# A decoder layer's rotary embedding: biases of queries and keys moved from TensorE products to a VectorE addition

## The reference

```python
def _rope(x):
    ...
    x_rot = jnp.concatenate([-x[..., d // 2:], x[..., :d // 2]], axis=-1)
    return x * jnp.cos(C) + x_rot * jnp.sin(C)
...
y = jnp.einsum('bte,fe->btf', x, W) + bias          # 16 heads of 32
q = _rope(proj(Wq, bq))
k = _rope(proj(Wk, bk))
v = proj(Wv, bv)
att = jnp.einsum('bhqd,bhkd->bhqk', q, k) / scale   # causal mask, softmax, times v, times Wo, + bo
...
x = x + self_attention(layernorm(x))
x = x + cross_attention(layernorm(x), ctx)          # q and output projections on rounded int8 values
x = x + experts(layernorm(x))                       # top 8 of 64, capacity 128
```

## Time and profile before

| | |
|---|---|
| median of three runs | 1581.28 us (1580.71, 1581.28, 1584.12) |
| profiled execution, its time | 1576.11 us |
| its span, first to last instruction | 1574.3 us |
| TensorE (PE) busy | 1423.6 us, 90% |
| VectorE (DVE) busy | 1134.7 us, 72% |
| ScalarE (ACT) busy | 971.0 us, 62% |
| GpSimd (POOL) busy | 673.4 us, 43% |
| chain that ended last | PE 66%, DMA 23% |
| granted TensorE clock, mean | 0.963 of full speed |

### The profile page before, as it was taken

How to read it: one execution, slowest core, us unless ns; L and a number is a source line. 1 busy time by engine, 2 the same in 40 slices (tenths; PEclk the granted TensorE clock), 3 DMA queues, 4 the chain that set the end, 5 groups by cost and what they waited for, 6 DMA issues and landing times.

```text
span 1574.3 us, 35702 instructions
## 1 busy us (share of the span) xinstructions
PE 1423.6 (90%) x11060; PEld 1074.5 (68%) x11060; DVE 1134.7 (72%) x3075; ACT 971.0 (62%) x3345; POOL 673.4 (43%) x655
## 2 busy tenths in 40 slices
PE   3689999999999999999999999999728888888895
PEld 2467777777777777777777777777516555555563
DVE  5568888888888888888888888888633444444453
ACT  3357777777777777777777777777614333333332
POOL 1012443534444434535344444344542545455556
PEclk9799999999999999999999999999859999999997
DMA  8771332222211110101100111100497999999964
GB/s 297 302 262 35 117 134 105 98 105 81 91 39 38 41 34 27 27 28 33 45 28 27 27 33 39 35 21 22 134 368 203 288 266 292 273 288 280 261 99 50
DMA packets 159882, 195.68 MB, mean 124 GB/s; under 512 B 39685, under 2 KB 122117, under 8 KB 159824
## 3 DMA queue, kind: packets, MB, share of 16 engines
q1 hardware_dynamic: 120912, 157.14, 30.4%
q0 software_dynamic: 38912, 37.87, 11.8%
HBM read 127.47 MB, written 130.29 MB: 164 GB/s over the span
## 4 chain that ended last, share of the span: by engine, by line
PE 66%; DMA 23%; issue 5%; DVE 3%; ACT 2%; POOL 1%; SPq 1%; POOLq 0%; DVEq 0%
PE bank L507 34%; DMA out<-x,slots 20%; PE bank L532 7%; PE bank L489 7%; PE bank L525 5%; PE bank L539 4%; PE bank L513 3%; PE bank L545 2%; PE bank L520 2%; DMA x_in<-in_x 1%; ACT probs L972 1%; PE bank L494 1%; POOL routed L1754 1%; DMA probsT<-in_kT_w 1%; DMA probsT<-in_oT_w 1%
## 5 line engine op out<-in xcount | busy, mean ns | idle before, releaser
L972 ACT ACTIVATE probs<-bank,small 128x128 f32<-128x128 f32 x1024 | 362.4, 378 | 51.2 <-DVE small L1276 47.9
L1754 POOL DMA_INDIRECT routed<-row,slots x248 | 253.4, 1022 | 132.8 <-issue 73.0
L1719 POOL TENSOR_TENSOR small<-small,half 128x1 f32<-128x1 f32 x96 | 54.5, 567 | 534.3 <-DVE small L1248 534.3
L1825 POOL DMA_INDIRECT out<-x,slots x128 | 198.6, 1551 | 193.3 <-DMA out<-x,slots 144.9
L972 ACT ACTIVATION_READ_ACCUMULATOR probs<-bank,small 128x1 f32 x1024 | 222.0, 217 | 0.0
L966 ACT ACTIVATE probsT<-bank 128x512 f32<-128x512 f32 x256 | 144.1, 612 | 102.3 <-PE bank L532 102.3
L1276 DVE TENSOR_REDUCE small<-bank 128x4 f32<-128x512 f32 x256 | 166.8, 683 | 32.3 <-PE bank L525 32.3
L532 PE MATMUL bank<-idf,probs 128*128 128x128 f32 x1024 | 146.6, 277 | 1.9 <-ACT probs L972 1.9
L1674 DVE TENSOR_SCALAR slots<-pairs 128x1 uint32<-128x1 f32 x128 | 13.7, 149 | 180.4 <-DMA out<-x,slots 176.8
L532 PEld LDWEIGHTS bank<-idf,probs 128*128 128x128 f32 x1024 | 122.0, 144 | 25.1 <-DVE probs L1285 3.0
L1206 ACT ACTIVATE xn<-bank 128x192 f32<-128x192 f32 x64 | 21.3, 332 | 149.3 <-PE bank L912 149.3
(11 more groups left out here) (244 smaller groups left out, 3845.7 us busy)
## 6 DMA issues: line engine op xcount, KB each, us to landing
w_gate_up<-in_w_gate SPq DMA_DIRECT2D x128, 192.0 KB, 3.6
w_gate_up<-in_w_up SPq DMA_DIRECT2D x128, 192.0 KB, 3.8
w_down<-in_w_down SPq DMA_DIRECT2D x128, 192.0 KB, 4.1
routed<-empty_row SPq DMA_DIRECT2D x4, 5120.0 KB, 22.8
x_in<-in_x SPq DMA_DIRECT2D x32, 256.0 KB, 2.6
ctx_sb<-in_ctxT_in SPq DMA_DIRECT2D x32, 256.0 KB, 3.0
x_res<-in_x SPq DMA_DIRECT2D x32, 256.0 KB, 2.6
out<-x SPq DMA_DIRECT2D x32, 256.0 KB, 2.0
```

Of the source, the lines that this page charges most:

```text
L972: last = act.activation(probs[:, g, j * P:(j + 1) * P], bank[:, b, j * P:(j + 1) * P], ACT.Exp, bias=negated[:, h:h + 1], **({"accum_out": ...
L1754: pool.indirect_dma_start(routed, bass.IndirectOffsetOnAxis(ap=slots_of(m)[:, k:k + 1], axis=0), row_of(m)[:, :], None, bounds_check=SLOTS ...
L1825: pool.indirect_dma_start(out.rearrange("b p (h c) -> (b p h) c", h=2), bass.IndirectOffsetOnAxis(ap=place_of[k % 2][:, half_:half_ + 1], ...
```

## The change

The bias goes into neither projection any more. In the setup each bias is loaded as one row spread over the 128 partitions and rotated for the 128 positions, into `turned_bias` (128x1024: queries, keys). In each tile's rotation the order of the products is turned round, and VectorE adds `turned_bias` to `rot` before the final sum. The rotation has five counted steps instead of four, so the counts of those who wait for it change. The selecting matrix, `bias_rows`, `pick`, their three DMAs, the four VectorE steps and GpSimd's cast go.

```diff
@@ load_biases (SyncE, setup)
-                sp.dma_start(xn2[:, :], biases).then_inc(s_bias, 16)
-                sp.dma_start(roped[:, 0:NB * P], bias_sel).then_inc(s_bias, 16)
-                sp.dma_start(pick[:, :], pick_t).then_inc(s_bias, 16)
+                for k, dst in enumerate((x1, x2)):
+                    sp.dma_start(dst[:, :], biases[k:k + 1].to_broadcast([P, D])).then_inc(s_bias, 16)
@@ project (TensorE)
-                steps = [(bias_of[:, BIASES.index(name), :], bias_rows[:, :])] if name in BIASES and piece == 0 else []
+                steps = []
@@ turn_keys, turn_cross_probs_2 (TensorE)
-                    reached(pe, d_rope, m, 4, 4)
+                    reached(pe, d_rope, m, 5, 5)
...
-                reached(pe, d_rope, m + 2, 4, 4)
+                reached(pe, d_rope, m + 2, 5, 5)
@@ rotate_pairs (VectorE)
-                dve.tensor_tensor(ro, qk, cos_sb[:, :].unsqueeze(1).to_broadcast([P, heads, DH]),
-                                  ALU.mult).then_inc(d_rope, 1)
                 dve.tensor_tensor(rt[:, :, 0:hd], qk[:, :, hd:DH],
                                   sin_sb[:, 0:hd].unsqueeze(1).to_broadcast([P, heads, hd]),
                                   ALU.mult).then_inc(d_rope, 1)
                 dve.tensor_tensor(rt[:, :, hd:DH], qk[:, :, 0:hd],
                                   sin_sb[:, hd:DH].unsqueeze(1).to_broadcast([P, heads, hd]),
                                   ALU.mult).then_inc(d_rope, 1)
-                until(dve, d_rope, nth(m, 4, 3))
+                dve.tensor_tensor(ro, qk, cos_sb[:, :].unsqueeze(1).to_broadcast([P, heads, DH]),
+                                  ALU.mult).then_inc(d_rope, 1)
+                until(dve, d_rope, nth(m, 5, 2))
+                dve.tensor_tensor(rot, rot, turned_bias[:, :], ALU.add).then_inc(d_rope, 1)
+                until(dve, d_rope, nth(m, 5, 4))
                 dve.tensor_tensor(roped[:, :], roped[:, :], rot, ALU.add).then_inc(d_rope, 1)
@@ setup (VectorE), between the second and third low part
-            dve.wait_ge(s_bias, 48)
-            both, hi_b, lo_b = (t[:, :] for t in (xn2, x1, x2))
-            chained(dve.tensor_copy(hi_b.bitcast(F32R), both))
-            chained(dve.tensor_tensor(lo_b, both, hi_b, ALU.subtract))
-            chained(dve.tensor_scalar(lo_b, lo_b, pick[:, 1:2], None, ALU.mult))
-            dve.scalar_tensor_tensor(out=bias_rows[:, :], in0=hi_b, scalar=pick[:, 0:1], in1=lo_b,
-                                     op0=ALU.mult, op1=ALU.add).then_inc(s_wprep, 1)
@@ setup (VectorE), after the sixth low part and the wait for the constants
+            dve.wait_ge(s_bias, 32)
+            for k, raw in enumerate((x1, x2)):
+                b, t, r = (a.rearrange("p (h d) -> p h d", d=DH)
+                           for a in (raw[:, :], xn2[:, :], turned_bias[:, k * D:(k + 1) * D]))
+                hd = DH // 2
+                dve.tensor_tensor(r, b, cos_sb[:, :].unsqueeze(1).to_broadcast([P, H, DH]), ALU.mult)
+                dve.tensor_tensor(t[:, :, 0:hd], b[:, :, hd:DH], sin_sb[:, 0:hd].unsqueeze(1).to_broadcast([P, H, hd]), ALU.mult)
+                chained(dve.tensor_tensor(t[:, :, hd:DH], b[:, :, 0:hd],
+                                          sin_sb[:, hd:DH].unsqueeze(1).to_broadcast([P, H, hd]), ALU.mult))
+                chained(dve.tensor_tensor(r, r, t, ALU.add))
@@ setup (GpSimd)
-            pool.wait_ge(s_bias, 48)
...
-                             (bias_of[:, :, :].rearrange("r i n -> r (i n)"), roped[:, 0:NB * P])):
```

More of the change, by code:

```diff
@@ L60 @@
 MASKED = -1e30
-BIASES = ("q", "k")
-NB = len(BIASES)
-N_INIT = 8
+N_INIT = 7
 RING = 16
@@ L105, in layer @@
 def layer(nc, x, ctxT_in, qT_w, kT_w, vT_w, oT_w, xkT_w, xvT_w, xq_w, xp_w, biases, vb, xkb, xvb, ob, xbq, xbp, routerT,
-          w_gate, w_up, w_down, cos_t, sin_t, ident_f, causal, prior, slot0, pick_t, bias_sel, out):
+          w_gate, w_up, w_down, cos_t, sin_t, ident_f, causal, prior, slot0, out):
     routed = nc.dram_tensor("routed", (SLOTS, ROW), F32).ap()
@@ L132, in layer @@
         slot_base = sb("slot_base", [P, E])
-        pick = sb("pick", [P, 2])
         v_bias = sb("v_bias", [P, KT])
@@ L186, in layer @@
             ctx_sb = early("ctx_sb", [P, D])
-            bias_rows = early("bias_rows", [P, D], F32R)
-            bias_of = early("bias_of", [P, NB, P], F32R)
+            turned_bias = early("turned_bias", [P, 2 * D])
             xv_bias = early("xv_bias", [P, D])
@@ L860, in turn_quantised_weights @@
                 for n, staged in enumerate((roped[:, :], packed[:, :])):
-                    pe.wait_ge(s_wprep, n + 2)
+                    pe.wait_ge(s_wprep, n + 1)
                     if n == 1:
@@ L869, in turn_quantised_weights @@
                     last.then_inc(s_wT, 1)
-                pe.wait_ge(s_wprep, 4)
+                pe.wait_ge(s_wprep, 3)
                 for g in range(KT):
@@ L885, in _ @@
             pe.wait_ge(s_lo_dve, 3)
-            pe.wait_ge(s_wprep, 1)
             pe.wait_ge(s_init, N_INIT)
@@ L1187, in _ @@
             act.wait_ge(s_const, 16 * N_CONST)
-            act.wait_ge(s_wprep, 5)
+            act.wait_ge(s_wprep, 4)
             act.wait_ge(s_init, N_INIT)
@@ L1649, in _ @@
             dve.tensor_scalar(xq_bs[:, :], xq_bs[:, :], SCALE, None, ALU.mult).then_inc(s_wprep, 1)
-            dve.wait_ge(s_wprep, 5)
+            dve.wait_ge(s_wprep, 4)
             dve.wait_ge(s_wT, 4)
@@ L1796, in _ @@
             pool.wait_ge(s_ident, 16)
-            pool.wait_ge(s_bias, 48)
             pool.wait_ge(s_const, 16 * N_CONST)
-            for dst, src in ((idb[:, :], idf[:, :]), (mask_add[:, :], x3T[:, 0:P]), (before[:, :], x3T[:, P:2 * P]),
-                             (bias_of[:, :, :].rearrange("r i n -> r (i n)"), roped[:, 0:NB * P])):
+            for dst, src in ((idb[:, :], idf[:, :]), (mask_add[:, :], x3T[:, 0:P]), (before[:, :], x3T[:, P:2 * P])):
                 pool.tensor_copy(dst, src).then_inc(s_init, 1)
@@ L1845, in tables @@
     p = np.arange(P)
-    of_bias = p[:, None] // 2 == np.arange(NB)[None, :]
     return {
@@ L1849, in tables @@
         "sin_t": np.concatenate([-sin, sin], 1).astype(np.float32),
-        "pick_t": (p[:, None] % 2 == np.arange(2)[None, :]).astype(np.float32),
-        "bias_sel": np.repeat(of_bias.astype(np.float32), P, axis=1),
         "ident_f": np.eye(P, dtype=np.float32),
@@ L1869 @@
         "xkT_w": wkv[:D].T, "xvT_w": wkv[D:].T, "xq_w": a["L0_xattn_wq"], "xp_w": a["L0_xattn_wp"],
-        "biases": np.pad(np.repeat(np.stack([a["L0_attn_bq"], a["L0_attn_bk"]]), 2, axis=0),
-                         ((0, P - 2 * NB), (0, 0))),
+        "biases": np.stack([a["L0_attn_bq"], a["L0_attn_bk"]]),
         "vb": a["L0_attn_bv"][by_place], "xkb": bkv[:D], "xvb": bkv[D:], "ob": a["L0_attn_bo"],
```

## The result

The changed kernel takes 1578.36 us (median of 22 runs, 1569.49 to 1583.25), the kernel before, timed beside it, 1582.48 us (22 runs, 1578.61 to 1589.61): a ratio of 0.9967, 95% interval 0.9955 to 0.9978. By the ratio that is some 5.2 us less (3.5 to 7.1), by the two medians 4.1. The forecast had 9.9 us less and 1571.4 us, with a range that ends at 1577.5: the sign was right, the size about half or less, the time just outside the range. The changed kernel's profiled execution took 1569.49 us, the shortest of its 22 runs, its span 1567.4 us (1574.3 before, 1564.4 forecast).

The account below looks back on a forecast made before the run. TensorE was taken to bound the tile loop, with VectorE off the path. Setup 4.3 us more and products 14.2 us less gave −9.9 us: 1566.2 profiled, 1571.4 us as median, range 1566.0 to 1577.5.

Parts of the forecast that it names:

- The two products: TensorE, each tile: two 128x512 products fewer; 60 that count at 0.236 us each, 14.2 us gained.
- rival 4: TensorE, loop: a removed product gives back only half its distance, 7.1 us gained, 2.8 net, 1578.5 us; chance 0.03.
- rival 1: Each tile: late rotation stalls TensorE by 0.15 us (1575.9 us, chance 0.12) or 0.25 us (1578.9, chance 0.06).
- The addition at nothing: VectorE, each tile's rotation: one more addition, 1.23 us, ends 0.12 us before TensorE needs it; stall taken as 0.
- Rivals 1 and 3: Late rotation stalls TensorE; or GpSimd and VectorE obstruct each other, 0.86 us a tile, 1597.2 us, the latter's chance 0.04.
- The setup: VectorE, before the attention bias: rotating both biases costs 4.3 us, all passed on through the fills to the x tile.
- The DMAs' bytes: Setup loads: three DMAs removed, two broadcast DMAs added, shifting the weight matrices by 0, ends ±0.5 us.
- Rival 2: Setup: price hidden if the x tile lands by total DMA load; the 4.3 us vanish, 1567.1 us; chance 0.08.
- The sum up to the last scatter: Setup plus tile loop: 4.3 us lost and 14.2 gained, together 9.9 us less.
- The stage of the experts after the tiles only starts earlier: After the tile loop: the experts' stage merely begins sooner, so the whole 9.9 us gain reaches the end.
- From the profile to the median: Whole kernel: the timed median lies 5.17 us above the profiled execution, so 1566.2 us becomes 1571.4.
- The range: Whole kernel's time: 1566.0 us, setup's price hidden, up to 1577.5, small TensorE stalls plus 0.5 us of setup and scatter.

Follow-up runs that it names:

- e5: Changed kernel with the addition of the turned biases made twice in every tile: 1609.76 us in one run, beside 1579.13 for the kernel before.
- the cut pair: Kernel before and changed kernel, both without the experts' stage and its weight loads, on chip 13: 1185.28 and 1174.45 us.
- e15: Changed kernel with the setup's bias rotation moved into VectorE's wait for the output bias sum: 1571.94 us against 1584.42 before, ratio 0.9920.

## Why the prediction was half right

- **The two products: right for each body, a little high as a sum.** The body was to be 32.92 us and is 32.93 to 32.94, in the first timing and on chip 13. From the x tile's landing to the last scatter the profiles gain 12.7 us (whole kernels) and 13.4 (cuts) of the 14.2 forecast; the last two distances between scatters gain nothing. By the 131 ns for a product that the Trainium skill gives ("TensorE: Matmul & The Clock Gate", back-to-back issue gap) the body would have been 33.13 us; the traces don't agree, and rival 4 is out. That the measured time lies beside rival 4's 1578.5 us and rival 1's 1578.9 is chance: neither mechanism is in the traces.
- **The addition at nothing: right**, by its own reason. It lasts 1.21 us in all 32 tiles, no wait for the rotation appears, and e5 gives the slack of 0.12 us back within 0.01. The wait before the second sum was to be 0.32 us and is 0.39. Rivals 1 and 3 are out where the body is short; no row shows the addition lengthened beside GpSimd.
- **The setup: the right mechanism, 1 us too small at the attention bias.** The turning was priced at 4.3 us and takes 4.24. The DMAs' bytes were put at 0, with ends of 0.5 us; the broadcast loads cost 0.7 to 0.8 us of later weights, and the attention bias came 5.05 us later. At the x tile 4.0 us were left in one pair and 5.9 in the other, as its DMA chanced to take 15.1 or 16.7 us, so that the landing at 96.3, forecast at 96.6, was luck. Rival 2 is out.
- **The sum up to the last scatter: right in the timing, high in the profiles.** 9.9 us were forecast; the cut pair has 10.8 by medians, the profiles 8.7 and 7.5. From first to last scatter 12.0 and 12.5 us were gained.
- **"The stage of the experts after the tiles only starts earlier": this step failed.** It took the stage's length from one profile as a constant. That length, 397.0 us, is the lowest of twelve, which go up to 408.7, so it can swallow or double a gain of 5 us in any comparison of two profiles. In the profiled pair it took 1.8 us back; in the first timing some 5.6 (by the ratio) to 6.7 (by the medians), if the attention stage gained there what it did on chip 13. Why the stage was longer there, by the change (A1) or by that job (A2), stays open; e15 favours A2.
- **From the profile to the median: this term failed too.** The forecast added the 5.2 us by which the median of before lay above its profiled execution. For the changed kernel that distance was 8.9 us (1578.36 and 1569.49). The profiled execution was forecast at 1566.2 and took 1569.5; the median missed by 7.0 us, 3.3 by the profiled execution and 3.7 by the distance. Both profiles are of lucky executions: the changed kernel's is the shortest of its 22 runs, and the one of before (1576.11) lies below all 22 of its timed ones (1578.61 and up). The stage of the experts is the likely source of the scatter, since the cuts without it scatter by 2 to 4 us in five runs each and whole kernels on the same chip by 9 to 10 in six and eleven, but no run isolates it.
- **The range was too narrow.** It allowed for half a microsecond of DMAs and some scatter. It should have held the stage behind the last scatter at several microseconds either way, and that on some chips TensorE is not what bounds the loop: there the sign turns (ratios 1.0023, 1.0049 and 1.0083), a case that no rival had.
- **Two slips that change nothing.** Without any overlap the turning comes to 4.6 us, not 4.8. And in the earlier trace rows the first of the two slowed products met not the GpSimd instruction that starts at 102.11 us but the one before it (L1729, 100.86 to 102.15), which reads out of SBUF as well.

## What to carry to other kernels

Work taken off the engine that bounds a loop is worth its full length only up to the next stage: where that is paced by DMAs, take its length from several runs, or leave it out of both kernels and compare what is left, as the cut pair did. Before calling added work hidden, add it once more; here 1.23 us beyond the first addition cost 1.10 us in each tile, which gave the slack within 0.01. A cause read from one profile wants a look at the same rows in the others: the slow products of e15 are in profiles without its early start as well. And time a change on more than one chip: here the same change is worth 0.3% in the first timing and costs 0.2 to 0.8% on three other chips.

## What was not expected of the hardware

- The same kernel takes 1579 to 1584 us on two of the chips and 1782 to 1789 us on four, by waits of VectorE in each body. There the loop absorbs work: 60 products less change nothing, and the whole change costs 3.6 to 14.5 us by medians.
- The same twelve products in the setup take 3.0 us in twelve traces and 4.8 to 5.2, mostly at 1.2 GHz, in eight, whether they begin at 53 or at 59 us.
- The x tile's load of 256 KB, asked for at 75 to 85 us behind the fills, takes anything from 13.7 to 17.4 us, a spread of nearly the whole price of the setup.
